# Attention rounds of a graph network: the last group but one's edge step and the last group's score step change places

## The reference

```python
xt = (x @ W.T + bias).reshape(n, H, C)
alpha = leaky_relu(alpha_src[row] + alpha_dst[col], 0.2)
amax = segment_max(alpha, col)
ex = exp(alpha - amax[col])
alpha = ex / (segment_sum(ex, col)[col] + 1e-16)
out = segment_sum(xt[row] * alpha[..., None], col)
```

## Time and profile before

| what | value |
|---|---|
| median of 3 runs | 4349.86 us (4349.19 to 4353.6) |
| the profiled execution | 4343.06 us |
| its span, first to last instruction | 4341.3 us |
| mean granted TensorE clock | 0.745 of full speed |
| POOL busy | 3081.9 us (71%) |
| DVE busy | 2539.8 us (59%) |
| PE busy | 2488.5 us (57%) |
| ACT busy | 860.6 us (20%) |

### The profile page before, as it was taken

The page is one execution under the profiler, slowest core; times in us unless marked ns, Lnnn a source line. Parts: engine busy times, 40 slices in busy tenths (PEclk is TensorE's granted clock), DMA queues, the critical chain, the costliest instruction groups (busy, mean ns, idle before and its releaser), DMA issues.

```text
span 4341.3 us, 72570 instructions
## 1 busy us (share of the span) xinstructions
PE 2488.5 (57%) x13901; PEld 2078.1 (48%) x13902; DVE 2539.8 (59%) x7085; ACT 860.6 (20%) x2948; POOL 3081.9 (71%) x3262
## 2 busy tenths in 40 slices
PE   8833444444444444444455676766677667667675
PEld 3333344433433434343344565655566556556564
DVE  7742334444434443444445777777777777777776
ACT  5400111101110111110112222222222222222222
POOL 2177777777777777777737777777777777777774
PEclk9956767767767677677666877778877787787777
DMA  9622222222222222222214222222222222222221
GB/s 322 258 54 55 62 63 59 65 60 62 63 60 64 60 62 63 60 65 61 61 41 115 56 59 62 59 59 62 60 62 60 59 62 60 62 60 60 62 59 44
DMA packets 192089, 314.95 MB, mean 73 GB/s; under 512 B 69617, under 2 KB 123233, under 8 KB 190948
## 3 DMA queue, kind: packets, MB, share of 16 engines
q0 software_dynamic: 103424, 215.33, 21.4%
q1 hardware_dynamic: 38907, 68.15, 4.6%
q10 hardware_dynamic: 49310, 26.90, 2.2%
HBM read 238.52 MB, written 71.59 MB: 71 GB/s over the span
## 4 chain that ended last, share of the span: by engine, by line
POOL 37%; issue 25%; PE 22%; DVE 9%; ACTq 3%; ACT 2%; DMA 1%; DVEq 0%; POOLq 0%; SPq 0%
POOL G L646 37%; PE bank L1773 9%; PE quad L1818 3%; ACTq L819 2%; PE quad L1824 2%; PE quad L1813 1%; DVE A L1302 1%; PE quad L1860 1%; DMA xt_table<-w_all 1%; PE quad L1715 1%; PE bank L1715 1%; PE bank L1716 1%; PE quad L1716 1%; ACT w_all L894 1%; DVE stats L198 1%
## 5 line engine op out<-in xcount | busy, mean ns | idle before, releaser
L646 POOL DMA_INDIRECT G<-rel_table,idx x1600 | 1517.8, 949 | 633.9 <-issue 487.5
L646 POOL DMA_INDIRECT G<-xt_table,idx x1616 | 1526.8, 945 | 545.1 <-issue 545.1
L1906 PEld LDWEIGHTS quad<-ident,top 128*128 128x128 f32 x3328 | 569.4, 269 | 199.1 <-issue 198.2
L1906 PE MATMUL quad<-ident,top 128*128 128x128 f32 x3328 | 582.1, 356 | 119.9 <-DVEq L1507 119.7
L1267 DVE SCALAR_TENSOR_TENSOR agg<-bank,sel,agg 128x128 f32 x208 | 63.7, 347 | 821.1 <-PE bank L1773 809.0
L1937 PE MATMUL bank<-M,onehot 128*128 128x132 f32 x3328 | 445.4, 290 | 167.5 <-DVE M L1556 163.1
L1937 PEld LDWEIGHTS bank<-M,onehot 128*128 128x128 f32 x3328 | 411.2, 199 | 199.3 <-issue 199.3
L1773 PE MATMUL bank<-G,M 128*128 128x128 f32 x1616 | 267.3, 343 | 292.4 <-issue 278.6
L1773 PEld LDWEIGHTS bank<-G,M 128*128 128x128 f32 x1616 | 263.5, 259 | 296.7 <-issue 296.7
L1922 PE MATMUL bank<-Z,w_all 128*128 128x8 f32 x832 | 160.2, 321 | 378.4 <-DVEq L1524 253.5
L957 ACT ACTIVATE M<-G,M 128x32 f32<-128x32 f32 x1664 | 363.9, 308 | 13.3
(11 more groups left out here) (324 smaller groups left out, 3521.3 us busy)
## 6 DMA issues: line engine op xcount, KB each, us to landing
side<-rel_table SPq DMA_DIRECT2D x4736, 0.5 KB
side<-xt_table SPq DMA_DIRECT2D x4736, 0.5 KB
rel_table<-G SPq DMA_DIRECT2D x98, 512.0 KB, 3.4
G<-rel_table,idx POOLq DMA_INDIRECT x1616, 2.6
G<-xt_table,idx POOLq DMA_INDIRECT x1616, 7.1
side<-rel_table ACTq DMA_DIRECT2D x1408, 0.5 KB
side<-xt_table ACTq DMA_DIRECT2D x1408, 0.5 KB
xt_table<-w_all ACTq DMA_DIRECT2D x23, 264.0 KB
```

Of the source, the lines that this page charges most:

```text
L646: g.indirect_dma_start(out=G[:, s, c, 0:width], out_offset=None, in_=table, in_offset=bass.IndirectOffsetOnAxis(ap=idx[:, s, c:c + 1], axi ...
L1906: ins = t.matmul(banks[j][:, hd * P:(hd + 1) * P], top[:, j, hd:hd + 1].to_broadcast([P, P]), ident[:, :], start=False, stop=(hd == HEADS ...
```

## The change

Only the round of group 101 is altered, on two queues. On DVE `edges(101)` comes before `scores(102)`. On PE `sums(101)` comes before `maxima(102)` and `turn_miss(102)`. No instruction is added or removed, and the waits inside each step stay with it. The steps of the Chain are counted in the new order.

```diff
@@ VectorE, round_of
-                if landed:
+                if landed and gr != MAIN - 2:
                     scores(groups, c, (s + 1) % SLOTS, 1 - k, landed)
                 edges(groups, c, gr, s, k, (lambda: merge(groups, c, gr - 1, gr - 1, last, 1 - k)) if last is not None else (lambda: None))
+                if landed and gr == MAIN - 2:
+                    scores(groups, c, (s + 1) % SLOTS, 1 - k, landed)
@@ TensorE, round_of
                 to_slots(groups, gr)
+                if gr == MAIN - 2:
+                    sums(groups, gr)
                 if more:
                     maxima(groups, gr + 1, 1 - k)
                     turn_miss(groups, gr + 1, 1 - k)
-                sums(groups, gr)
+                if gr != MAIN - 2:
+                    sums(groups, gr)
```

## The result

The changed kernel takes 4356.51 us (median of 22 runs, 4351.8 to 4359.26), the kernel before 4350.52 us (22 runs, 4347.16 to 4353.6). The ratio is 1.0015, with a 95% interval of 1.0009 to 1.0021: 3.9 to 9.1 us slower, 6.0 us by the medians. The forecast was 4356.3 us, +6.4. It held that a loss under 0.2% can't be told from no change; with 22 runs of each, the interval lies above 1. Two executions of later versions, 4504 us with 34 added matmuls and 8347 us with 18, at mean granted clocks of 0.53 and 0.55, are left out of all ratios as slow ones.

The account below looks back on a forecast made before the run. POOL's gathers set the pace over most of the program, then a bare dependency chain bounds the last 43 us. Terms +6.7 - 0.3 = +6.4 us on 4349.86 gave 4356.3 us, range 4350 to 4361.

Parts of the forecast that it names:

- Where the end is set: After POOL's last gather: the last 43 us are a bare dependency chain on DVE, with PE near the end.
- (1): DVE, round of group 101: `edges(101)` starts at 4299.9 and not at 4302.31, 2.4 us earlier.
- (2): DVE: `scores(102)` behind `edges(101)` takes 1.3 us; `tops` could start at 4310.6, on DVE alone a gain of 1.0 us.
- (3): PE before `tops(102)`: `sums(101)`, `miss` and `top` matmuls form one burst of 10.95 us; `tops(102)` starts 6.7 us later.
- (4): After `tops(102)` starts: `hit` is covered by 1.8 us and `to_slots(102)` by at least 1.1 us, so distances stay.
- (5): PE, `sums(102)` at the end: 5.0 us at half clock in place of 5.7, -0.3 us, bounds -1.1 to 0.
- Half clock throughout: Rival, PE's burst before `tops(102)`: stays at 1.2 GHz, 16.6 us long; total +12.1, 4361.9 us; chance 0.10.
- A gain: Rival, PE between `M` of group 101 and `tops(102)`: maxima stay hidden, -1.3 us, 4348.6 us; chance 0.06.
- the loss be caught up: Rival, PE: `sums(102)` finds full clock (-2.5), the new burst finds it at 3.4 us (-0.8); +3.4, 4353.3; chance 0.12.

Follow-up runs that it names:

- 22 fillers: Kernel before plus 22 identity matmuls, into a bank nothing reads, on PE ahead of `sums(102)`: last gather to end 42.73 us against 43.01, ratio 1.0000.
- 16 fillers: Changed kernel plus 16 identity matmuls, into a bank nothing reads, on PE ahead of `sums(101)`: last gather to end 46.72 us against 49.07, ratio 1.0010.
- filled waits: Kernel before with `merge(100)` moved into DVE's wait for the last gather and `finish` into that for `sums(102)`: last gather to end 39.99 us, ratio 0.9996.

## Why the prediction was right

- *Where the end is set.* A chain after the last gather, with nothing of the steady rounds in it: confirmed by the distances, which moved with the edits in this stretch (but for the 22 fillers that ended too early). The last gather began anywhere from 4297.21 to 4305.57. The late starts stand mostly with slower versions, but the changed kernel's two profiles, 7.5 us apart there, have the same distance within 0.2 us.
- *(1) `edges(101)` starts earlier.* Foreseen 4299.9, measured 4299.02 in the time of before, since `to_slots(101)` ran at full clock, 1.03 us and not 1.85 as in the earlier trace rows. That was luck, as nothing in the change reaches it: the granted clock was 1.00 from 4300.00 to 4305.81, through 4.18 us of idle time and `to_slots(101)`, and fell just after (0.54 over the next 0.39 us). In the versions with the `miss` matmuls ahead and with 16 fillers `to_slots(101)` took 1.84 us, and `edges(101)` started 1.09 us after `fade_arg`, where 1.1 was foreseen. Of these 0.9 us in the changed kernel 0.35 us were lost again: the idle time ahead of `merge(100)` is 0.73 us, not 0.38, in every version with this order on VectorE; why is open. `M` was 0.5 us earlier than foreseen.
- *(2) `scores(102)` behind `M`.* Right in its own length, wrong in what follows: after it DVE executes nothing for 1.50 us, before the first step of `nodes(102)`, where I had put 0.26. DVE's queue is not idle in them. It reads two block numbers from `plan` into registers (`load_block`, line 423), and these stand in the code behind the release of `top` and ahead of `nodes(102)`. Two lines for this stretch, after and then before (count; shortest, median and longest in ns; starts of the first and the last):

```profile
L423 DVEq TENSOR_LOAD <-plan x2: 298/306/313, 4316.0 to 4316.6; - x2
L423 DVEq TENSOR_LOAD <-plan x2: 299/303/307, 4309.1 to 4309.7; - x2
```

After, they start when the reduction of `top` has ended (4315.87). Before, they ran under the three slices of `M` (4309.02 to 4310.90) and cost nothing. The term could be read from the trace of before, in the round of 101, where the short steps of `prepare` stand in front:

```profile
4294.01 0.23 DVE L1516 TENSOR_SCALAR Z<-am,sel 128x8 f32 x1 [1.50 <-issue]
```

So DVE was ready for `tops` at about 4318.16, 4311.2 in the time of before, and even with free maxima the new order would have gained 0.4 us and not 1.0. The wait for PE hid this slip.
- *(3) The burst.* Work at full clock 8.45 us foreseen, 8.55 measured where the clock was full. At half clock 5.0 us foreseen, 5.9 measured, 0.2 outside the bound from the earlier trace rows; but a us at half clock cost 0.44 us and not 0.5, so the price was 2.6 us against 2.5. The two errors nearly cancel. The product of duration and clock, taken as the work at full clock, fails in the same: 6.66 x 0.57 = 3.8 for `sums`, not 4.12. The four `miss` matmuls took 1.03 us at full clock in the second profile, not half of 1.87. Burst 10.95 foreseen, 11.16 measured, so `tops(102)` came 6.32 us later in place of 6.7: the earlier start outweighed the longer half clock.
- *(4) The covers.* `hit` 2.2 us ahead of `Z` (1.8 foreseen), and 1539 did not wait. When `finish` was taken away, 1539 waited 0.27 us for `to_slots(102)`, the low end of what that version's expectation allowed.
- *(5) The last sums.* -0.3 foreseen, -0.28 measured, by luck: the term was a mean of other bursts, and the change does nothing to this one. After 9.1 to 9.2 us of idle time it took 6.66 and 6.55 us in the two profiles of before, 6.38 and 6.41 in those of the changed kernel, and 5.88 to 6.16 in three other versions.
- *The rivals.* Half clock throughout did not come: the full clock was back 5.9 us into the burst. (Its 16.6 us don't follow from the prediction's own terms either: twice 8.45 is 16.9.) A gain is refuted from both halves: each order alone loses. That the loss be caught up did not happen, the last sums started at half clock as before.

So the result is +6.06 us in the distance against +6.4, by the named mechanism. That the absolute forecast, 4356.3, lies 0.2 us from the median is luck: the interval of the loss is 3.9 to 9.1 us, and the kernel before was itself 0.7 us slower in 22 runs than in the three that the forecast started from. What the clock costs was read in part from other bursts; only the run with the fillers shows it apart. Why the clock comes back after 5.9 us in one burst and sooner in others stays open.

## What to carry to other kernels

An idle stretch of one engine is not there to be filled by the first thing that is ready. Ask what the postponed instruction releases: here 1.0 us of `scores` let another engine begin work that was covered only because it began first. Put work that nothing waits for into the stretch (a merge, an output), and keep in front whatever starts another engine. When a difference is smaller than the spread of executions, measure a distance inside the trace from the last event that the edit can't touch, and take more than one profile where the clock can fall differently. When the trace says "issue", look at what the engine's queue itself executes there: here it was two register loads, free behind long work and exposed behind short work.

## What was not expected of the hardware

- After the 22 fillers TensorE idled for 4.25 us and the last sums began at half clock (6.48 us). After 3.32 us they ran at full clock in one execution (4.12 us); in another of the same kernel they began at full clock, and it fell inside the burst (5.79 us). After 2.50, 1.56 and 1.31 us they, or the burst of `sums(101)`, ran at full clock from start to end. `to_slots(101)`, after 4.15 to 4.22 us of idle time, took 1.03 us in both profiles of the changed kernel, 1.53 us in one version and 1.84 to 1.85 us in the others.
- Two register loads on DVE's queue, some 0.6 us each with their register work, add nothing behind the slices of `M` and 1.50 us behind the short steps of `scores` or `prepare`. In the versions with VectorE's order of before, `nodes(102)` follows `M` at once (4308.74 with filled waits). The position in the code fits this: the loads stand behind a release that waits for the last short step, whereas the slices of `M` release by themselves. No version moved the loads.
- The part of the program ahead of the last gather, the same in both kernels, took between 4297.21 and 4305.57 us in the profiles, a spread larger than what any edit did.
